# One ring of seven PSUM banks for the attention stages, and their layer norms finished on GpSimd

## The chip, the core and the metric

The kernel runs on one core of one Trainium2 chip. The metric is device time in microseconds (us), the median of several runs. A core has TensorE (PE, the matmuls; its weight loads are shown apart as PEld), VectorE (DVE), ScalarE (ACT), GpSimd (POOL) and SyncE (SP, which here only issues DMAs). The core's PSUM, where matmuls put their results, has eight banks, and a bank holds 128 x 512 float32 numbers, which is one tile of this kernel.

## What is computed

Three transformer layers act on x of shape (4, 512, 288) (batches, tokens, channels), and a rotation stands between the second and the third. Cut to what matters:

```python
h = modulate(layernorm(x), shift, scale)                 # norm 1
q, k, v = split(h @ w_qkv + b_qkv)                       # 16 heads of 18 channels
attn = softmax(einsum('bqhd,bkhd->bhqk', q, k) * 18 ** -0.5)
x = x + gate * (einsum('bhqk,bkhd->bqhd', attn, v).reshape(x.shape) @ w_proj + b_proj)
h = modulate(layernorm(x), shift2, scale2)               # norm 2
x = x + gate2 * mlp(h)       # layer 0: mixture of 4 experts, top 2; layers 1 and 2: one MLP, 288 -> 1152 -> 288
# between layers 1 and 2:
U, _ = qr(P); R = expm(skew(silu(cond) @ W.T + b))
x = x + (x @ U @ R - x @ U) @ U.T
```

The QR factorisation is done by 64 Householder reflections, one after the other.

## The kernel before

**Stages.** Each of the three layers has a start (norm 1, q and k of batch 0, first row maxima), then the attention of four batches, then the MLP of the four batches. Attention and MLP do not overlap except for a few steps at the border.

**A batch of attention.** The 16 heads form four groups of four (g = 0..3), and the 512 keys form four blocks (kt = 0..3), so a batch has 16 steps (g, kt). `walk` sets the order of a step for all engines: two heads' tiles, place A, the other two heads' tiles, place B, the value products, place C. A step has four score tiles (`score_tiles`, L783; ScalarE takes each out with an exp, L1150) and four maximum tiles (`max_tiles`, L770; VectorE reduces each to a row maximum, L1486). The maxima belong to the group after the next (g + 2), so that from g = 2 on they are those of the next batch. The negated maxima are transposed (`turn_maxima`, "R", L697), copied by ScalarE to `nmT`, and written by DMA (L394) as two more rows of `qs`, so that the score matmul itself subtracts the maximum. `value_products` (L794) uses bank 4.

**Other work.** `other_work` lists what stands at the places A, B and C: tiles of q and k of the next batch ("P", five tiles, L683: ScalarE takes the high part out, L1105, VectorE the low part, L1468), v ("V"), transposes of the attention's output ("on", "ot"), the projection ("pj", L734), transposes of normalised tokens ("T1", "T2", L723), the steps of the norms on VectorE ("LN1a" to "LN1h" for the next batch, "LN2a" to "LN2h" for the batch before), and in layer 0 the matrix exponential ("X"), the gate logits, and the reflections ("HH": GpSimd computes, PE sums over partitions, L636, ScalarE copies, L1078, GpSimd goes on, L529 to L540 and L524 to L520). A P tile goes through DRAM: SP stores it (`store_tile`, L369), waits for the store, and loads it in another layout as `qs` and `ks` (`stack`, L386). SP does all of this and the nmT DMAs in one queue, in order.

**Banks.** Scores use banks 2 and 3 in turn, maxima 0, 1 and 5, other work 6 and 7, value products 4. PE waits before a tile until the tile that was last in its bank is read: a score for the exp two scores before, a maximum for the reduction three maxima before, other work for the one two before it. In the MLP banks 0 to 2 and 4 to 7 are used for the hidden and output tiles, and 3 is spare.

**Norms.** A norm on VectorE has 25 instructions: four sums (L1312) and four aggregations (L1315), three to get a first guess of the inverse root, nine Newton steps on 128 x 4 numbers (L1321 to L1323), four normalisations of 128 x 288 (L1330), and a copy of 128 x 384 (L1334), most of them with a wait for the one before.

## Time and profile before

| | us |
|---|---|
| median of 3 runs | 2026.04 (2024.82 to 2034.39) |
| the profiled execution | 2024.0 |
| its span | 2022.2 |
| PE busy | 1818.6 (90%) |
| DVE busy | 1216.9 (60%) |
| ACT busy | 951.0 (47%) |
| POOL busy | 421.2 (21%) |

The span is that of one execution. A busy PE is not PE at its peak: a matmul row also holds the time it spends in the pipeline (0.39 to 0.50 us where the next one starts 0.23 us later), so waits are better read from the distance between the starts of rows than from the busy time. PEclk is the granted clock, 1.00 for 2.4 GHz and 0.50 for 1.2 GHz.

### The profile page before, as it was taken

What the parts mean: (1) busy time and instruction counts of PE and PEld (TensorE: products, weight loads), DVE (VectorE), ACT (ScalarE), POOL (GpSimd) and SP (SyncE); (2) the same over time, 40 slices, a digit from 0 to 9 for tenths busy, and PEclk for the clock granted to TensorE, in tenths of its full rate; (3) what the DMA queues carried; (4) which work ended last, traced back from release to release, by engine and by line L of the source; (5) the groups of instructions that cost most, each with busy time, mean ns of one, the idle gap of its engine ahead of it and who ended that gap; (6) DMA issues with size and microseconds to landing.
All of it is one profiled execution on the core that took longest, in us unless ns stands there. A gap on an engine that the chain in (4) does not pass through costs nothing.

```text
span 2022.2 us, 29597 instructions
## 1 busy us (share of the span) xinstructions
PE 1818.6 (90%) x10184; PEld 1186.3 (59%) x10184; DVE 1216.9 (60%) x2635; ACT 951.0 (47%) x1676; POOL 421.2 (21%) x1066
## 2 busy tenths in 40 slices
PE   5798999998999999999688898989987788888998
PEld 4352445445898998998443444448863344434697
DVE  3654777755455464556576777735546677775544
ACT  2144555555444454444145565564431555556543
POOL 0001444555566663444100000000000000000000
PEclk9678989889999999999688999979996889999899
DMA  6335221203011020100222222111003222221100
GB/s 193 108 86 144 83 61 60 63 22 110 1 31 34 1 65 1 64 1 0 87 66 80 68 70 67 53 62 52 1 1 115 73 64 73 65 80 50 49 13 36
DMA packets 69964, 118.95 MB, mean 59 GB/s; under 512 B 8144, under 2 KB 31451, under 8 KB 69780
## 3 DMA queue, kind: packets, MB, share of 16 engines
q1 hardware_dynamic: 65348, 105.00, 16.5%
q0 software_dynamic: 2064, 8.80, 1.8%
q10 hardware_dynamic: 2416, 3.42, 0.5%
q8 instruction: 74, 1.21, 0.2%
q14 instruction: 62, 0.51, 0.1%
HBM read 85.28 MB, written 31.73 MB: 58 GB/s over the span
## 4 chain that ended last, share of the span: by engine, by line
PE 64%; DVE 12%; DMA 9%; SPq 6%; ACT 4%; issue 4%; POOL 0%; DVEq 0%; ACTq 0%
PE ps L913 17%; PE ps L924 16%; DMA qk_rows<-qk 6%; PE ps L794 6%; PE ps L783 6%; DVE mx L1486 5%; PE ps L683 4%; PE ps L734 3%; SPq L386 3%; ACT pT L1150 2%; PE ps L770 2%; PE ps L723 2%; DMA qs<-nmT 1%; PE ps L690 1%; SPq L394 1%
## 5 line engine op out<-in xcount | busy, mean ns | idle before, releaser
L1486 DVE TENSOR_REDUCE mx<-ps 128x1 f32<-128x512 f32 x768 | 485.5, 682 | 131.0 <-PE ps L770 122.5
L1150 ACT ACTIVATE pT<-ps 128x512 f32<-128x512 f32 x768 | 416.2, 593 | 301.9 <-PE ps L783 295.1
L770 PE MATMUL ps<-ks,qs 54*128 54x512 f32 x768 | 337.7, 523 | 72.9 <-DMA ks<-qk_rows 50.6
L783 PE MATMUL ps<-qs,ks 56*128 56x512 f32 x768 | 319.9, 493 | 62.5 <-ACT pT L1150 35.1
L1432 DVE TENSOR_TENSOR gl<-gf,gh 128x512 fp32r<-128x512 f32 x216 | 149.9, 695 | 272.4 <-ACT gh L1073 269.9
L1072 ACT ACTIVATE gf<-ps,cols 128x512 f32<-128x512 f32 x216 | 148.8, 689 | 339.9 <-PE ps L913 339.5
L783 PEld LDWEIGHTS ps<-qs,ks 56*128 56x128 f32 x768 | 129.1, 197 | 273.4 <-ACT pT L1150 142.2
L924 PE MATMUL ps<-w2h,gh 128*128 128x288 f32 x864 | 255.7, 296 | 1.6 <-DVE tmpx L1519 1.3
L924 PE MATMUL ps<-w2h,gl 128*128 128x288 f32 x864 | 254.7, 295 | 0.0
L924 PE MATMUL ps<-w2l,gh 128*128 128x288 f32 x864 | 254.1, 294 | 0.0
L794 PE MATMUL ps<-pT,vaug 128*32 128x512 f32 x1536 | 228.0, 663 | 0.0
L770 PEld LDWEIGHTS ps<-ks,qs 54*128 54x128 f32 x768 | 136.4, 206 | 121.9 <-DVE mx L1486 64.0
L913 PE MATMUL ps<-hTh,w1h 128*128 128x512 f32 x432 | 177.1, 410 | 1.8 <-DVE w1l L1455 1.7
L913 PE MATMUL ps<-hTl,w1h 128*128 128x512 f32 x432 | 170.9, 396 | 0.0
L913 PE MATMUL ps<-hTh,w1l 128*128 128x512 f32 x432 | 170.8, 395 | 0.0
L924 PEld LDWEIGHTS ps<-w2h,gh 128*128 128x128 f32 x864 | 162.2, 188 | 11.3 <-DVE tmpx L1519 2.2
L924 PEld LDWEIGHTS ps<-w2l,gh 128*128 128x128 f32 x864 | 162.8, 188 | 8.3
L924 PEld LDWEIGHTS ps<-w2h,gl 128*128 128x128 f32 x864 | 162.3, 188 | 0.0
L1073 ACT ACTIVATE gh<-ps,cols 128x512 fp32r<-128x512 f32 x216 | 147.2, 681 | 0.0
L1468 DVE SCALAR_TENSOR_TENSOR qk<-ps,cols,qk 126x512 fp32r<-126x512 f32 (+1 forms) x60 | 44.9, 749 | 87.3 <-ACT qk L1105 86.3
L529 POOL TENSOR_TENSOR hs<-hR,hs 96x1 f32<-96x1 f32 x64 | 39.6, 619 | 275.0 <-ACT hR L1078 275.0
L913 PEld LDWEIGHTS ps<-hTh,w1h 128*128 128x128 f32 x432 | 81.7, 189 | 19.7 <-issue 6.4
(206 smaller groups left out, 2649.0 us busy)
## 6 DMA issues: line engine op xcount, KB each, us to landing
qk_rows<-qk SPq DMA_DIRECT2D x96, 252.0 KB
qs<-qk_rows SPq DMA_DIRECT2D x96, 144.0 KB
ks<-qk_rows SPq DMA_DIRECT2D x96, 144.0 KB
...
```

Of the source, the lines that this page charges most:

```text
L386: sp.dma_start(to[at:at + part.shape[0], i % 2, 2 * g:2 * g + 2, :].bitcast(F32), part).then_inc(S[f"stack_ld{g}"], 16)
L683: ins = mm(ps[0:rows, n, :], w[:, c, o:o + rows], h[:, c, :], start=(c == 0 and k == 0), stop=(c == KC - 1))
L770: ins = mm(bank(MAX_BANKS[v % 3]), qs[at:at + KMAX, buf, h // 2, qt * P:(qt + 1) * P], ks[at:at + KMAX, buf, h // 2, :], start=True, stop= ...
L783: ins = mm(bank(2 + i % 2), ks[at:at + KROW, b % 2, h // 2, kt * P:(kt + 1) * P], qs[at:at + KROW, b % 2, h // 2, :], start=True, stop=Tru ...
L794: ins = mm(ps[32 * i:32 * i + 32, 4, :], vaug[:, kt, g % NG * HG + i, :], pT[:, kt % 2 * HG + i, :], start=(kt == 0), stop=(kt == TT - 1), ...
L913: ins = mm(bank(j % 3), w[:, c, o:o + P], h[:, c, :], start=(c == 0 and n == 0), stop=(c == KC - 1))
L924: ins = mm(ps[:, 4 + t, 0:C], g[:, j % 3, t * P:(t + 1) * P], w[:, j, :], start=(j == 0 and n == 0), stop=(j == NJ - 1 and n == 2))
L1072: A(gf[:, j % 3, :], bank(j % 3), gelu, bias=bias).then_inc(S["gf_done"], 1)
L1073: A(gh[:, j % 3, :], bank(j % 3), gelu, bias=bias).then_inc(S["gh_done"], 1)
L1150: A(pT[:, kt % 2 * HG + i, :], bank(2 + i % 2), ACT.Exp, scale=SCALE).then_inc(S["exp_done"], 1)
L1432: V.tensor_tensor(gl[:, j % 3, :], gf[:, j % 3, :], gh[:, j % 3, :].bitcast(F32), ALU.subtract).then_inc(S["gl_done"], 1)
L1486: V.tensor_reduce(mx[:, g % NG, qt, column(i):column(i) + 1], bank(MAX_BANKS[(NU * g + qt * HG + i - first) % 3]), AX.X, ALU.max).then_inc ...
```

## The change

- **Banks.** `banks()` hands out the seven banks 6, 7, 0, 1, 5, 2, 3 in one ring to scores, maxima and other work, in the order in which PE issues them. A tile waits for the reader of the tile seven takes before, whatever it was. The end of a layer's attention uses 5, 6, 7.
- **Norms.** Within attention VectorE keeps `bn_stats` and `bn_aggr` (`statistics`). GpSimd does the rest (`normalise`): add epsilon, power -0.5, two products on 128 x 4, four 128 x 288 `tensor_scalar`, the copy of 128 x 384. These are 18 norms: norm 1 of batches 1 to 3 and norm 2 of batches 0 to 2, in each layer. Norm 1 of batch 0 and norm 2 of batch 3 stay on VectorE.
- **GpSimd's order.** In layer 0 it now walks through the same places as the others, so reflections, norms and the issue of three weight loads stand in that order. Reflections in attention are at steps 0, 2, 5, 7, 10, 12 and 14 of batches 1 and 2 and at the first six of these in batch 3 (20 in all; before at every even step, 24), and the third expert gets three a batch where it had two.
- **Tiles of q and k.** P2 stays at step 8 (g = 2, kt = 0), P3 moves from step 12 to 11, P4 from step 0 of the next batch to step 15; for batch 0 P4 is computed in the start, among the maxima.
- **Negated maxima.** They are laid out so that two DMAs of two rows each replace four of one row.
- The wait for all readers (`all_read`) at the end of a start is gone.

```diff
-FWD_KT = (0, 2)
-FWD_J = ((1, 4, 7), (1, 4, 7), (2, 6), (2, 6))
-FWD_AT = (B - 1) * NG * len(FWD_KT)
+FWD_STEP = ((), (0, 2, 5, 7, 10, 12, 14), (0, 2, 5, 7, 10, 12, 14), (0, 2, 5, 7, 10, 12))
+FWD_J = ((1, 4, 7), (1, 4, 7), (1, 4, 7), (2, 6))
+FWD_AT = sum(len(s) for s in FWD_STEP)
...
+def banks():
+    table, ring, n = {}, [0], [AROUND]
+    def take(phase, kind, key):
+        table[phase, kind, key] = n[0][ring[0] % len(n[0])]
+        ring[0] += 1
...
+            def tile(g, kt, which):
+                for i in which:
+                    take(phase, "score", (g, kt, i))
+                    if g + 2 < NG or b + 1 < B:
+                        take(phase, "max", (g + 2, kt, i))
...
-MAX_BANKS = (0, 1, 5)
+AROUND = (6, 7, 0, 1, 5, 2, 3)
+BANK = banks()
...
-                    for row in range(2):
-                        for e in range(2):
-                            at = HALF * e + KMAX + row
-                            sp.dma_start(qs[at:at + 1, G // NG % 2, 2 * g:2 * g + 2, :].bitcast(F32),
-                                         nmT[HG * row + 2 * e:HG * row + 2 * e + 2, :].bitcast(F32)).then_inc(S[f"nm_ld{g % 2}"], 16)
+                    for e in range(2):
+                        at = HALF * e + KMAX
+                        sp.dma_start(qs[at:at + 2, G // NG % 2, 2 * g:2 * g + 2, :].bitcast(F32), nmT[HG * e:HG * e + HG, :].bitcast(F32)).then_inc(S[f"nm_ld{g % 2}"], 16)
...
+            def normalise(which, i, b, eps, xn_free):
...
+                pool.wait_ge(S[f"mv{which}_ready"], TT * done)
+                ordered(g.tensor_scalar(var, mvp[:, which - 1, :, 1], eps, 1.0, ALU.add, ALU.mult))
+                ordered(g.tensor_tensor(y, var, power[:, :].to_broadcast([P, TT]), ALU.pow))
+                ordered(g.tensor_tensor(w, mean, y, ALU.mult))
+                ordered(g.tensor_scalar(w, w, -1.0, 1.0, ALU.mult, ALU.mult))
...
+                for t in range(TT):
+                    g.tensor_scalar(xn[:, t, 0:C], xres[:, b * TT + t, :], y[:, t:t + 1], w[:, t:t + 1],
+                                    ALU.mult, ALU.add).then_inc(S[f"xn{which}_ready"], 1)
...
-                        pe.wait_ge(S["exp_done"], G * NU + (NU * g + kt * HG + i + 1))
+                        n = bank_free("score", (g, kt, i), "exp_done", G * NU + (NU * g + kt * HG + i + 3))
...
-                            layernorm(1, it + 1, b + 1, EPS[l], kind[3], (S["tr2_done"], it * KC + KC))
+                            statistics(1, it + 1, b + 1, kind[3])
```

On PE, in a step without other work (layer 1, batch 1, g = 3, kt = 2), where L783 is a score, L770 a maximum and L794 the value products; before:

```order
L783 MATMUL ps<-qs,ks 128x512 [waits exp_done]
L770 MATMUL ps<-ks,qs 128x512 [waits mx_done]
L783 MATMUL ps<-qs,ks 128x512 [waits exp_done]
L770 MATMUL ps<-ks,qs 128x512 [waits mx_done]
L783 MATMUL ps<-qs,ks 128x512 [waits exp_done]
L770 MATMUL ps<-ks,qs 128x512 [waits mx_done]
L783 MATMUL ps<-qs,ks 128x512 [waits exp_done]
L770 MATMUL ps<-ks,qs 128x512 [waits mx_done]
L794 MATMUL ps<-pT,vaug 32x512 [waits exp_done]
```

and the same step after, where L880, L867 and L891 are the same three (on_ready is VectorE's division of the attention's output, nmT_ready ScalarE's copy of the maxima):

```order
L880 MATMUL ps<-qs,ks 128x512 [waits mx_done]
L867 MATMUL ps<-ks,qs 128x512 [waits nmT_ready]
L880 MATMUL ps<-qs,ks 128x512 [waits exp_done]
L867 MATMUL ps<-ks,qs 128x512 [waits mx_done]
L880 MATMUL ps<-qs,ks 128x512 [waits exp_done]
L867 MATMUL ps<-ks,qs 128x512 [waits mx_done]
L880 MATMUL ps<-qs,ks 128x512 [waits on_ready]
L867 MATMUL ps<-ks,qs 128x512 [waits exp_done]
L891 MATMUL ps<-pT,vaug 32x512 [waits exp_done]
```

The matmuls and their order are the same; what each waits for is now the tile seven takes back, of either kind or of other work.

On VectorE, in steps 1 and 2 of the same batch (L1486 is a maximum, L1498 a tile of v, L1315 and the rest the norm); before:

```order
L1498 TENSOR_TENSOR vaug<-ps,vbias 128x16x18 [waits pv_done,v_mm]
L1315 BN_AGGR mv<-stats 128x2 x4
L1316 TENSOR_SCALAR nwt<-mv 128x4 [waits ln1_step]
L1318 TENSOR_SCALAR nwt<-nwt 128x4 [waits ln1_step]
L1319 TENSOR_SCALAR nwt<-nwt 128x4 [waits ln1_step]
L1486 TENSOR_REDUCE mx<-ps 128x1 [waits ln1_step,max_mm]
L1486 TENSOR_REDUCE mx<-ps 128x1 [waits max_mm]
L1498 TENSOR_TENSOR vaug<-ps,vbias 128x16x18 [waits pv_done,v_mm]
L1321 TENSOR_TENSOR nwt<-nwt 128x4
L1322 SCALAR_TENSOR_TENSOR nwt<-nwt 128x4 [waits ln1_step]
L1323 SCALAR_TENSOR_TENSOR nwt<-nwt 128x4 [waits ln1_step]
L1486 TENSOR_REDUCE mx<-ps 128x1 [waits ln1_step,max_mm]
```

and after, where L1614 is the tile of v, L1450 the aggregation and L1601 the maximum:

```order
L1614 TENSOR_TENSOR vaug<-ps,vbias 128x16x18 [waits pv_done,v_mm]
L1450 BN_AGGR mvp<-stats 128x2 [waits ln1_step,xc1_ready]
L1450 BN_AGGR mvp<-stats 128x2 x3
L1601 TENSOR_REDUCE mx<-ps 128x1 [waits max_mm] x2
L1614 TENSOR_TENSOR vaug<-ps,vbias 128x16x18 [waits pv_done,v_mm]
L1601 TENSOR_REDUCE mx<-ps 128x1 [waits max_mm] x2
```

The small steps between the maxima are gone from VectorE's queue.

On GpSimd, in batch 1 of layer 0, after the change (L594 to L604 are the norm, L567 and L568 begin the next reflection, whose end is not shown):

```order
L594 TENSOR_SCALAR nwp<-mvp 128x4 [waits mv2_ready]
L595 TENSOR_TENSOR nwp<-nwp,power 128x4 [waits lnp_step]
L596 TENSOR_TENSOR nwp<-mvp,nwp 128x4 [waits lnp_step]
L597 TENSOR_SCALAR nwp<-nwp 128x4 [waits lnp_step]
L601 TENSOR_SCALAR xn<-xres,nwp 128x288 [waits tr1_done,tr2_done,lnp_step]
L601 TENSOR_SCALAR xn<-xres,nwp 128x288 x3
L604 COPY xn<-xn 128x4x96 [waits xn2_ready]
L567 TENSOR_TENSOR hs<-hR,hs 96x1 [waits hh_cp]
L568 TENSOR_SCALAR hs<-hR 96x1 [waits hh_step]
```

Before, the reflections followed each other there with nothing between them.

## Rows read from the trace of the kernel before

**Rows 1.** Windows: layer 0 batch 1, its MLPs; layer 1 start and four batches.
```profile
core 0: us, PE busy (x) PEld busy (x) DVE busy (x) ACT busy (x) POOL busy (x), PEclk, DMA share, GB/s
...
196.70:295.80 99.10, 93.49 (x569) 47.33 (x565) 74.07 (x174) 52.47 (x101) 46.07 (x124) 0.93 0.29 84
...
520.00:960.00 440.00, 437.00 (x2590) 391.81 (x2589) 237.87 (x458) 200.50 (x335) 239.15 (x580) 1.00 0.07 23
966.60:1016.80 50.20, 30.23 (x79) 16.60 (x78) 30.64 (x56) 8.63 (x12) 0.22 (x2) 0.62 0.30 96
1016.80:1103.60 86.80, 73.98 (x404) 34.94 (x404) 58.40 (x131) 45.77 (x83) 0.00 (x0) 0.86 0.25 77
1103.60:1186.60 83.00, 72.91 (x411) 34.98 (x411) 65.09 (x150) 48.59 (x89) 0.00 (x0) 1.00 0.24 73
1186.60:1274.90 88.30, 78.63 (x411) 37.12 (x411) 65.37 (x150) 48.60 (x89) 0.00 (x0) 0.92 0.21 68
1274.90:1345.00 70.10, 63.65 (x326) 27.55 (x326) 37.05 (x85) 42.56 (x79) 0.00 (x0) 0.87 0.19 63
```

**Rows 2.** Timeline of PE, end of layer 1 batch 1: start us, us, engine line.
```profile
1178.64 0.50 PE L783 MATMUL ps<-qs,ks 56*128 56x512 f32 x1
...
1178.99 0.39 PE L783 MATMUL ps<-qs,ks 56*128 56x512 f32 x1
1179.83 0.50 PE L783 MATMUL ps<-qs,ks 56*128 56x512 f32 x1 [0.45 <-ACT pT L1150]
...
1180.75 1.07 PE L794 MATMUL ps<-pT,vaug 128*32 128x512 f32 x8
1181.75 0.49 PE L783 MATMUL ps<-qs,ks 56*128 56x512 f32 x1
...
1186.62 0.50 PE L783 MATMUL ps<-qs,ks 56*128 56x512 f32 x1 [1.71 <-DMA qs<-nmT]
```

**Rows 3.** Waits over the whole span: us in total, times, longest us.
```profile
PE ps L770 <- DMA ks<-qk_rows: 50.6, 12, 10.9
...
PE ps L783 <- ACT pT L1150: 35.1, 66, 1.4
...
PE ps L770 <- DVE mx L1486: 22.0, 33, 1.3
```

**Rows 4.** VectorE's groups in layer 1 batch 1: busy us, mean ns, idle before.
```profile
L1486 DVE TENSOR_REDUCE mx<-ps 128x1 f32<-128x512 f32 x64 | 40.7, 683 | 4.7 <-PE ps L770 3.4
...
L1330 DVE TENSOR_SCALAR xn<-xres,mv,nwt 128x288 f32<-128x288 f32 x8 | 3.0, 423 | 0.2 <-DVE nwt L1323 0.2
...
L1322 DVE SCALAR_TENSOR_TENSOR nwt<-nwt 128x4 f32<-128x4 f32 x6 | 1.0, 163 | 0.9 <-DVE nwt L1321 0.3
...
L1334 DVE COPY xn<-xn 128x384 f32<-128x384 f32 x2 | 0.7, 360 | 0.1
```

**Rows 5.** Chain that ended last, end of layer 1 batch 1: start us, us, what.
```profile
1171.43 1.85 PE ps L683 x7
...
1174.90 4.82 DMA qk_rows<-qk
...
1182.79 0.64 SPq L394
...
1184.71 1.87 DMA qs<-nmT
```

**Rows 6.** Timeline of GpSimd, one reflection in layer 0 batch 2.
```profile
301.66 0.55 POOL L529 TENSOR_TENSOR hs<-hR,hs 96x1 f32<-96x1 f32 x1 [3.64 <-ACT hR L1078]
...
305.66 0.46 POOL L510 TENSOR_TENSOR hp<-hr,hvc 96x165 f32<-96x165 f32 x1
...
308.42 0.30 POOL L520 TENSOR_TENSOR hr<-hp 96x55 f32<-96x55 f32 x1
```

**Rows 7.** VectorE's groups: MLP of layer 0 (GpSimd busy), then layer 1 (idle).
```profile
L1432 DVE TENSOR_TENSOR gl<-gf,gh 128x512 fp32r<-128x512 f32 x125 | 86.6, 694 | 155.6 <-ACT gh L1073 155.2 <-DVE stats L1312 0.2
...
L1432 DVE TENSOR_TENSOR gl<-gf,gh 128x512 fp32r<-128x512 f32 x30 | 20.7, 691 | 47.1 <-ACT gh L1073 47.1
```

236 lines of the change are left out of this document (156 added, 80 removed), and 9 rows, old and new, of the table own.

## The prediction

> **What bounds the kernel now.** First the windows by stage [rows 1]. In the MLPs of layer 0 TensorE is busy 437 of 440 us at the full clock, with a quarter of VectorE's time to spare: nothing there can be gained by this change, and the MLPs of the other layers look the same. In attention the row of layer 1, batch 1 is the one to read, because its clock is 1.00 throughout: 83.0 us, TensorE busy 72.9, VectorE 65.1, ScalarE 48.6. No engine is full, and 72.9 is an upper figure, since a matmul's row holds pipeline time. Batch 2 does the same work in 88.3 us at a clock of 0.92; batch 3, which prepares no next batch, takes 70.1.
>
> Why no engine is full is seen in a step that has nothing but tiles and value products [rows 2]. Two scores, with a maximum beside each, start at 1178.64 and 1178.99, so a pair costs TensorE 0.35 us. The third score starts at 1179.83, not at 1179.34: it waited for the exp that reads its bank. The next step starts at 1181.75, so the step took 3.11 us. TensorE's own part is 4 x 0.35 + 1.00 (value products, 1180.75 to 1181.75) = 2.40 us. VectorE's part is four reductions of 40.7 / 64 = 0.64 us [rows 4], 2.54 us. So the step costs 0.57 us more than its busiest engine needs. The two banks of the scores are what couples them. In the list of waits the same shows as 35.1 us behind exps and 22.0 us behind reductions [rows 3]; both understate it, since the row of the matmul before covers part of each wait.
>
> The third kind of wait is for DMA: 50.6 us for ks, 12 times, up to 10.9 us [rows 3], and 1.71 us at the border of batches 1 and 2, for the negated maxima [rows 2]. Its chain [rows 5]: P3 starts at 1171.43, its store is on its way from 1174.90 for 4.82 us, then come the loads, and at 1182.79 the first of four nmT DMAs, each 0.6 us of SP; the last lands at 1186.58. From P3 to the score are 15.2 us.
>
> **Part 1, the ring of banks.** Nothing is added: the matmuls and their order stay. In a bare step a score may now run 3.5 pairs ahead of the exps instead of 2, and a maximum about as far as before. Both ends: all of the 0.57 us in each of 16 steps, 9.1 us a batch; or nothing in the steps with other work, where ScalarE and VectorE catch up meanwhile, which leaves about 5 bare or nearly bare steps, 2.9 us. Steps with other work also stall today, so I take a value above the middle of 2.9 and 9.1: 6.1 less 0.6 for steps that VectorE or ScalarE fill by themselves (T1, the residuals), 5.5 us. Nine batches (0 to 2 of each layer): 49.5 us. Batch 3 has half its maxima and waits mostly for exps: 5 us each, 15 us. Sum 64.5, between 26 + 6 and 82 + 27.
>
> The coupling is new in one respect: a score may wait for a reduction, and a maximum for an exp. VectorE's queue is the longer one, 65.1 us a batch against 48.6 [rows 1], so scores could be held by it. This is where part 2 helps.
>
> **Part 2, the norms.** VectorE loses per batch eight normalisations (3.0 us), two copies (0.7), eighteen Newton steps (18 x 0.16 = 2.9) and six other small ones of about the same length (1.0) [rows 4]: 7.6 us, which leaves 57.5. It also loses the waits between them (0.9 us before L1322). On the path this is worth little beyond part 1, which already lets the waits for reductions go. Between 0 and 2.4 us a batch (22.0 us of waits over nine batches), I take 0.5: 4.5 us.
>
> GpSimd's price has no row of its own. A tensor_tensor of 96 x 165 takes 0.46 us and one of 96 x 55 0.30 us [rows 6], so 1.45 ns for an element more and 0.64 us for 288; for the copy of 384, 0.78 us. The power takes about the 0.55 us of L529, which is one; the three other small steps at most as much. A norm is then 4 x 0.64 + 0.78 + 4 x 0.55 + 0.4 for waits = 5.9 us. It starts at place C of step 1 and is needed by T1 at step 4, two steps later, 2 x 83.0 / 16 = 10.4 us now and 9.4 if the batch shrinks to 75; norm 2 has from step 7, place B, to step 9, place C. In layer 0 a reflection stands ahead of it in GpSimd's queue: 301.66 to 308.72, 7.1 us [rows 6]. With the 1 us until ScalarE's copy that is 7.1 + 1 + 5.9 = 14.0 us from place B of step 0, against 3.5 steps of 99.1 / 16 = 6.2 us, 21.7 us. So the norm costs nothing on the path. If the cover were gone each microsecond over it would cost 9 us a norm kind.
>
> Do the two engines hinder each other? VectorE's L1432 reads two SBUF tensors and takes 694 ns where GpSimd works beside it and 691 ns where it is idle [rows 7]. That is no hindrance. The Trainium skill (SBUF — State Buffer, "Who interferes with whom") says that a VectorE instruction with two SBUF inputs and a GpSimd instruction that reads SBUF lock each other out for a whole instruction. The row does not bear it out for GpSimd's short steps; by the rule some eleven such VectorE instructions a batch would each lose at most one 0.64 us GpSimd instruction, 7 us, and part 2 would give VectorE nothing. The skill also calls GpSimd the wrong place for elementwise work, about twice as slow for two inputs (GPSIMD Engine Reference, "4.1 Engine selection"); from VectorE's 0.42 us [rows 4] that is 0.85 us an instruction and 6.9 us a norm, which the cover still holds.
>
> **Part 3, P3, P4 and two DMAs for four.** P3 starts a step earlier (3.1 us) and SP issues two nmT DMAs fewer (2 x 0.6 = 1.2 us). Together they exceed the 1.71 us of the border's wait [rows 2]; what is late next is VectorE. Nine borders, 1.3 us each (the others wait less or more): 12 us, between 0 and 15. A P tile costs TensorE 1.85 us [rows 5] wherever it stands; only in a start does moving it pay. There the clock is 0.62 [rows 1], so P4 costs 3 us or more, and it now lies among maxima, where VectorE is the slow one. With the 1.2 us of DMA issues: 4 us, three starts, 12 us (3 to 15).
>
> **Part 4, what comes back.** The chain from P1 to the maxima of the next batch is of the same kind as that from P3, 15 us, and nothing shortens it. P1 is in step 5 and its load is needed in step 8. As steps 5 to 7 get shorter TensorE arrives sooner and waits longer for ks; in batch 0 all that these steps gain is lost. I put 2 us on each of nine batches, with the slower clock after such a wait: -18 us (0 to -40).
>
> **Reflections.** The attention has 20 for 24 and a spacing of 2 or 3 steps for 2; the third expert has a reflection each 10 us, as the first two have today in the 437 of 440 us [rows 1]. No cost.
>
> **Sum.** 64.5 + 4.5 + 12 + 12 - 18 = 75 us. The profiled execution took 2024.0 us (span 2022.2); 1949 us. The median of three is 2 us above that execution: 1951 us.
>
> **Rivals.**
> *More comes back through the clock.* The same work cost 5.3 us more at 0.92 than at 1.00 [rows 1]. If fewer waits keep the clock up, about 4 us more in ten batches, and part 1 at its upper end: 1951 - 45 = 1906 and below.
> *DMA takes over.* Steps 8 to 11 and 11 to 15 shrink too, and the chains of P2 and P3 (15 us each) become the pace: four steps at 3.8 us are 15.2 us. Then two more places in each of nine batches wait for 2 us: 1951 + 36 = 1987. For it: 50.6 us are waited for ks already. Against: only batch 0 waits long.
> *It doesn't do what it says.* The chain is PE, exp, value products, and the ring only moves the wait to the exps that the value products need: then only part 3 is left, 2 to 10 us, about 2018.
> *Slower: the clock falls.* The wait before a maximum is spread today; if it gathers at the DMA waits, the 1.2 GHz stretch that follows each of them in the starts (clock 0.62) comes in every batch. At 5.3 us for 0.08 of clock, ten batches at 0.78 in place of 0.92 cost 93 us, against the 75 gained: about 2044. It decides from a mean clock in attention below about 0.81.
>
> **How the numbers follow.** Forecast (1915 to 1975) 0.61; more through the clock (1880 to 1915) 0.10; DMA takes over (1975 to 2012) 0.16; no effect 0.06; slower 0.07. The range 1903 to 1993 leaves out most of the first rival's far half, the far half of the second, and the last two. A measurement can tell about 0.5%, 10 us, from no change. Faster by more: 0.61 + 0.10 + 0.16 = 0.87; within: 0.06; slower: 0.07.
>
> **What would show it.** A batch at full clock of 74 to 77 us for 83.0. A bare step of 2.6 to 2.8 us for 3.11, bound by reductions that follow each other without a gap. VectorE's busy time in such a batch near 57.5 us, and GpSimd with two norms of about 6 us. The border's wait gone. The wait for ks larger than 50.6 us. MLPs unchanged. The prediction is wrong if PE waits for xn at T1, if VectorE's reductions get longer than 0.68 us beside GpSimd, or if the clock in attention is lower than now.

## The result, and the profile after

The changed kernel takes 1898.45 us (median of 4 runs, 1893.26 to 1903.29) where the kernel before took 2025.43 us beside it (2018.41 to 2034.39): a ratio of 0.937, 95% interval 0.9326 to 0.9415. It is 127 us faster, where 75 were forecast; the direction was right, and the time lies 4.5 us below the low end of the range, 1903. The profiled execution has a span of 1896.5 us and a mean granted clock of 0.942, where the kernel before had 2022.2 us and 0.923.

First the page of the changed kernel: busy time and share of each engine, with the number of instructions. GpSimd has 81 us more than before, VectorE 68 us less, TensorE 95 us less, though its matmuls in attention are the same; the granted clock is higher, and how much of the 95 us is clock and how much is waiting inside its rows was not separated.

```profile
PE 1723.5 (91%) x10184; PEld 1165.3 (61%) x10184; DVE 1148.8 (61%) x2329; ACT 940.4 (50%) x1676; POOL 502.0 (26%) x1229
```

Windows of the changed kernel, the same stretches as in [rows 1]: the MLPs of layer 0, then layer 1: the start and its four batches. Columns: busy us (and instructions) of PE, PEld, DVE, ACT, POOL, then the granted clock.

```profile
510.00:945.00 435.00, 430.55 (x2570) 388.19 (x2568) 234.82 (x452) 197.80 (x331) 262.85 (x642) 1.00 0.07 23
945.00:993.80 48.80, 26.50 (x84) 15.96 (x84) 30.09 (x54) 9.30 (x13) 0.00 (x0) 0.66 0.30 99
993.80:1069.10 75.30, 68.93 (x406) 35.42 (x406) 54.31 (x114) 44.16 (x83) 4.41 (x9) 0.88 0.29 89
1069.10:1140.90 71.80, 69.31 (x417) 34.31 (x413) 57.66 (x117) 47.86 (x90) 8.78 (x18) 1.00 0.26 84
1140.90:1212.80 71.90, 69.18 (x415) 34.22 (x411) 57.54 (x117) 47.74 (x90) 8.78 (x18) 1.00 0.26 84
1212.80:1269.20 56.40, 52.68 (x322) 24.60 (x320) 31.81 (x68) 37.30 (x73) 4.39 (x9) 0.94 0.20 66
```

The row to compare is again batch 1 of layer 1, with a clock of 1.00 on both sides: 83.0 us have become 71.8. That is 11.2 us at the same clock, where the terms of the sum came to 5.3 (5.5 + 0.5 + 1.3 - 2). Batch 2 fell further, 88.3 to 71.9, since its clock also went from 0.92 to 1.00.

A bare step of that batch, PE and then VectorE (start us, us, engine, line; L880 is a score, L867 a maximum, L891 the value products, L1601 a reduction):

```profile
1134.11 0.50 PE L880 MATMUL ps<-qs,ks 56*128 56x512 f32 x1
1134.11 0.73 PE L867 MATMUL ps<-ks,qs 54*128 54x512 f32 x2
...
1135.73 1.06 PE L891 MATMUL ps<-pT,vaug 128*32 128x512 f32 x8
1136.72 0.50 PE L880 MATMUL ps<-qs,ks 56*128 56x512 f32 x1
...
1134.68 3.30 DVE L1601 TENSOR_REDUCE mx<-ps 128x1 f32<-128x512 f32 x5 [0.19 <-PE ps L867]
```

From 1134.11 to 1136.72 are 2.61 us, for 3.11 in [rows 2], and the five reductions follow each other without a gap. No wait for an exp is left in the step.

GpSimd's norm 1 in the same kernel, and then what TensorE waited for over the whole span (us in total, times, longest), PE's rows first and then three of the weight loads (L880 is a score, L867 a maximum):

```profile
1078.68 0.19 POOL L594 TENSOR_SCALAR nwp<-mvp 128x4 f32<-128x4 f32 x1 [69.77 <-DVE mvp L1450]
1078.95 1.02 POOL L595 TENSOR_TENSOR nwp<-nwp,power 128x4 f32<-128x4 f32 x1
...
1080.65 2.27 POOL L601 TENSOR_SCALAR xn<-xres,nwp 128x288 f32<-128x288 f32 x4
1082.99 0.50 POOL L604 COPY xn<-xn 128x384 f32<-128x384 f32 x1
```

```profile
PE ps L867 <- DMA ks<-qk_rows: 59.8, 13, 10.9
PE ps L880 <- DMA qs<-nmT: 19.1, 5, 7.1
PE ps L824 <- POOL xn L601: 5.4, 3, 2.0
PEld ps L880 <- DVE mx L1601: 34.3, 66, 0.8
PEld ps L880 <- ACT pT L1251: 19.7, 29, 1.1
PEld ps L867 <- DVE mx L1601: 15.3, 48, 0.7
```

The norm takes 4.8 us from 1078.68 to 1083.49 (5.9 forecast). The wait for ks has grown from 50.6 us [rows 3], and TensorE waits three times for GpSimd's xn, once in batch 3 of each layer. Now that all share a ring, the weight loads of scores wait for reductions too (34.3 us), which none did before; this is the new coupling that the prediction named.

### The profile page after: what moved, and what is told of

Its sections match the earlier page's. It is cut to its first block, busy times and chain, and to the rows that moved or that the text cites. A ratio compares the mean times of both kernels' runs of the same rounds, so it can differ in the third digit from the quotient of the medians.

```text
span 1896.5 us, 29159 instructions
## 1 busy us (share of the span) xinstructions
PE 1723.5 (91%) x10184; PEld 1165.3 (61%) x10184; DVE 1148.8 (61%) x2329; ACT 940.4 (50%) x1676; POOL 502.0 (26%) x1229
## 4 chain that ended last, share of the span: by engine, by line
PE 71%; DMA 9%; DVE 6%; ACT 5%; SPq 4%; issue 3%; POOL 2%; ACTq 0%; DVEq 0%; POOLq 0%
PE ps L1014 18%; PE ps L1025 17%; PE ps L891 6%; PE ps L880 6%; DMA qk_rows<-qk 6%; PE ps L784 4%; PE ps L867 3%; PE ps L791 3%; SPq L426 2%; PE ps L835 2%; DVE mx L1601 2%; ACT pT L1251 1%; PE ps L805 1%; DMA ks<-qk_rows 1%; PE ps L824 1%
## 5 line engine op out<-in xcount | busy, mean ns | idle before, releaser
L1601 DVE TENSOR_REDUCE mx<-ps 128x1 f32<-128x512 f32 x768 | 482.4, 681 | 96.6 <-PE ps L867 94.5
L1251 ACT ACTIVATE pT<-ps 128x512 f32<-128x512 f32 x768 | 409.4, 598 | 242.7 <-PE ps L880 241.8
L867 PE MATMUL ps<-ks,qs 54*128 54x512 f32 x768 | 292.0, 491 | 62.8 <-DMA ks<-qk_rows 59.8
L880 PE MATMUL ps<-qs,ks 56*128 56x512 f32 x768 | 272.7, 462 | 21.8 <-DMA qs<-nmT 19.1
L880 PEld LDWEIGHTS ps<-qs,ks 56*128 56x128 f32 x768 | 119.4, 194 | 182.0 <-issue 107.2
L891 PE MATMUL ps<-pT,vaug 128*32 128x512 f32 x1536 | 214.2, 624 | 10.0 <-ACT pT L1251 10.0
L594 POOL TENSOR_SCALAR nwp<-mvp 128x4 f32<-128x4 f32 x18 | 3.5, 195 | 824.9 <-DVE mvp L1450 824.8
L867 PEld LDWEIGHTS ps<-ks,qs 54*128 54x128 f32 x768 | 124.4, 202 | 97.8 <-DMA ks<-qk_rows 64.8
L567 POOL TENSOR_TENSOR hs<-hR,hs 96x1 f32<-96x1 f32 x64 | 39.2, 612 | 208.5 <-ACT hR L1179 208.5
L1014 PEld LDWEIGHTS ps<-hTh,w1l 128*128 128x128 f32 x432 | 81.9, 190 | 19.8
```

The costliest lines, as they stand in the source:

```text
L867: ins = mm(bank(n), qs[at:at + KMAX, buf, h // 2, qt * P:(qt + 1) * P], ks[at:at + KMAX, buf, h // 2, :], start=True, stop=True, tile_posi ...
L880: ins = mm(bank(n), ks[at:at + KROW, b % 2, h // 2, kt * P:(kt + 1) * P], qs[at:at + KROW, b % 2, h // 2, :], start=True, stop=True, tile_ ...
L891: ins = mm(ps[32 * i:32 * i + 32, 4, :], vaug[:, kt, g % NG * HG + i, :], pT[:, kt % 2 * HG + i, :], start=(kt == 0), stop=(kt == TT - 1), ...
L1014: ins = mm(bank(j % 3), w[:, c, o:o + P], h[:, c, :], start=(c == 0 and n == 0), stop=(c == KC - 1))
L1251: A(pT[:, kt % 2 * HG + i, :], bank(BANK[when[0], "score", (g, kt, i)]), ACT.Exp, scale=SCALE).then_inc(S["exp_done"], 1)
L1601: V.tensor_reduce(mx[:, g % NG, qt, column(i):column(i) + 1], bank(BANK[when[0], "max", (g, qt, i)]), AX.X, ALU.max).then_inc(S["mx_done"], 1)
```

## Where the time went, by batches

From the trace of each kernel the first score of every batch was taken, and for the end of batch 3 the first matmul of the MLP; the sums of the three layers are below, in us. The kernels between are experiments, told of below; from row to row one part is added (with the norms also the new places of the reflections and the start without `all_read`, which no run takes apart). It is one execution of each kernel; the ratios, given with the experiments, differ from this by up to some 9 us in a step.

| | batch 0 (3) | batches 1, 2 (6) | batch 3 (3) | all |
|---|---|---|---|---|
| before | 282.4 | 543.0 | 225.9 | 1051.3 |
| + norms on GpSimd (e4) | 279.9 | 499.2 | 228.3 | 1007.4 |
| + places of P, two DMAs (e1) | 269.6 | 484.9 | 219.2 | 973.7 |
| + scores and maxima share five banks (e15) | 266.0 | 486.2 | 199.1 | 951.3 |
| + all seven in one ring (changed kernel) | 259.8 | 467.5 | 195.0 | 922.3 |

The norms give 44 us, the places and DMAs 34, the sharing of five banks 22, the ring of seven 29: 129 us together. About 2.4 us of it are given back in the third expert of layer 0, which has a reflection more in each batch (eight matmuls in all). Its windows, before and then after, have their PE columns beside a clock of 1.00:

```profile
728.90:846.60 117.70, 117.70 (x702) 106.25 (x701) 64.03 (x119) 53.36 (x89) 54.05 (x130) 1.00 0.09 28
...
704.10:824.20 120.10, 118.76 (x710) 107.13 (x709) 63.87 (x118) 54.75 (x93) 77.57 (x193) 1.00 0.09 28
```

## Experiments: the parts alone and taken away

All ratios are to the kernel before on the same chip; 0.01 is 20 us. The changed kernel has 0.937. Theory A said that the ring carries the gain, theory B that ring and relieved VectorE need each other.

**Old banks.** In `banks()`, each kind has its own banks again:

```diff
-        table[phase, kind, key] = n[0][ring[0] % len(n[0])]
+        own = {"score": (2, 3), "max": (0, 1, 5)}.get(kind, (6, 7))
+        table[phase, kind, key] = own[used[own] % len(own)]
```

> The changed kernel with the banks dealt out as before: scores on 2 and 3, maxima on 0, 1 and 5, other work on 6 and 7; norms on GpSimd and all else as changed. Theory A (the ring carries the gain, the rest is small): 2000 us or more, that is over 100 us slower than the changed kernel, and a full-clock batch of 81 to 83 us for 71.8. Theory B (ring and relieved VectorE need each other; each alone gives a part): 1960 to 1990 us, batch at 76 to 80. By the prediction's own terms (64.5 us for the ring) 1963 us. A bare step of about 3.1 us again by all of them.

Measured: 1954.37 us, ratio 0.9621 (0.9597 to 0.9645). The whole ring is worth 51 us as the last part to be added (0.9621 - 0.937 = 0.0251). That is the prediction's term less a fifth, and half of what theory A wanted; what the ring loses again by later waits for ks (part 4 of the prediction) is inside the 51. The batch 1 of layer 1 takes 74.8 us, not 81.

**Norms on VectorE.** `on_gpsimd` gives False, `layernorm` with its parts a to h stands at its old places, `normalise` is not called.

> The changed kernel with the 18 norms of attention wholly on VectorE, in the places that they had before; the ring and all else as changed. Theory A: 1903 to 1915 us, since the norms were priced at 0.5 us a batch. Theory B: VectorE's 7.6 us a batch come back nearly whole, as its reductions are what the steps wait for once the ring is there: 9 x 5 to 7.6 us, plus clock, 1945 to 1975 us, with waits for mx and a batch of 77 to 79 us.

Measured: 1962.57 us, ratio 0.9642 (0.9616 to 0.9668). The norms are worth 55 us as the last part, where 4.5 were forecast. Theory A falls here. In its trace TensorE also waits for VectorE's xn, 16.1 us in 8 places (7.9 us in 9 places in the kernel before, none in that of the norms alone, below).

**The ring alone, and the norms alone.** The first has the edit of e2, the old places of P3 and P4 and four DMAs; the second the old banks, places and DMAs.

> The ring of seven banks alone: norms on VectorE, P3 at step 12, P4 at step 0 of the batch itself, four one-row DMAs for the negated maxima, all as before; only the reflections stand at their new steps. Theory A: 1925 us or less (over 100 of the 127 us gained). Theory B: 1955 to 1985 us. By the prediction's terms 2024 - 64.5 = 1960 us.

> The norms on GpSimd alone: banks, places of P3 and P4 and the four DMAs as before. Theory A: 2015 to 2025 us. Theory B: 1995 to 2012 us, since the waits for reductions (22 us) and the serial steps of the norm go. By the prediction's terms 2020 us.

Measured: the ring alone 2003.13 us, ratio 0.9868 (0.984 to 0.9896), 27 us; the norms alone 1980.56 us, ratio 0.9742 (0.9724 to 0.976), 52 us. Both theories thought too well of the ring, and both too little of the norms alone. Of the ring alone, batch 3, which has no norm 1 and few maxima, has 23.6 us (225.9 to 202.3); the six batches in the middle have 8 (543.0 to 534.9). Theory B is right in that much of the ring's gain there needs the norms gone, and wrong in that the norms need no ring: they give 52 us by themselves.

**P3 and P4 at their old places, four DMAs for two.** The first puts P3 back to step 12 and P4 to step 0, with SyncE's order that belongs to them (its edit is not shown); the second is:

```diff
-                        at = HALF * e + KMAX
-                        sp.dma_start(qs[at:at + 2, ...], nmT[HG * e:HG * e + HG, :])
+                        for r in range(2):
+                            at = HALF * e + KMAX + r
+                            sp.dma_start(qs[at:at + 1, ...], nmT[HG * e + 2 * r:HG * e + 2 * r + 2, :])
```

> The changed kernel with P3 at step 12 and P4 at step 0 of the batch itself again (and SyncE's order that belongs to them); ring, norms on GpSimd and two DMAs as changed. Theory C (the places are worth what they showed beside the old banks, where norms alone gave 1981 us and norms with new places 1954 us): 1925 to 1935 us, steps 0, 12 and 15 of a batch longer by about 4 us together. Theory D (by the prediction's term, 1.3 us a border and 3 of the 4 us of a start): 1898 + 12 + 9 = 1919 us or less.

> The changed kernel with four one-row DMAs for the negated maxima instead of two of two rows. Theory C: 1904 to 1912 us, 1.2 us more at a border where the maxima are late and in a start, hidden elsewhere. Theory D: 1898 to 1903 us.

Measured: old places 1939.23 us, ratio 0.9562 (0.9513 to 0.9611), 39 us; four DMAs 1911.17 us, ratio 0.9412 (0.9366 to 0.9459), 9 us, which is not clear of noise, since this interval overlaps with that of the changed kernel. Beside the ring the places are worth more than both theories gave them: in the trace of e5 TensorE waits 45.3 us in 16 places for qs<-nmT, and 19.1 in 5 places in the changed kernel. Beside the old banks, from e4 to e1, places and DMAs together are worth 0.0121, 25 us, by the ratios the forecast of 24 (34 us by the single traces above).

## Experiments: why the norms were worth so much

The prediction held 22.0 us of waits behind reductions [rows 3] for an upper bound. The wait list has PE's rows and PEld's rows, and only the first were read. The weight load of the same maximum stands in the page of the kernel before with three times as much (idle time and what ended most of it, at the end of the line), and so does that of a score:

```profile
L770 PEld LDWEIGHTS ps<-ks,qs 54*128 54x128 f32 x768 | 136.4, 206 | 121.9 <-DVE mx L1486 64.0
L783 PEld LDWEIGHTS ps<-qs,ks 56*128 56x128 f32 x768 | 129.1, 197 | 273.4 <-ACT pT L1150 142.2
```

Neither number is a price. The 22.0 us count too little, since the matmul before covers part of a wait; the weight loads' rows count too much: scores wait 142.2 us for exps there, and the ring alone (e3), which leaves 21.5 us of it, gave 27 us. The price has to be read in the steps.

Step 9 of layer 1, batch 1, before, shows what happens: two weight loads of maxima on PEld, and VectorE in the same stretch.

```profile
1158.02 0.18 PEld L770 LDWEIGHTS ps<-ks,qs 54*128 54x128 f32 x1 [1.05 <-DVE mx L1486]
...
1160.82 0.18 PEld L770 LDWEIGHTS ps<-ks,qs 54*128 54x128 f32 x1 [1.55 <-DVE mx L1486]
```

```profile
1157.27 1.29 DVE L1486 TENSOR_REDUCE mx<-ps 128x1 f32<-128x512 f32 x2
1158.48 0.15 DVE L1321 TENSOR_TENSOR nwt<-nwt 128x4 f32<-128x4 f32 x1
1158.78 0.16 DVE L1322 SCALAR_TENSOR_TENSOR nwt<-nwt 128x4 f32<-128x4 f32 x1
1159.09 0.17 DVE L1323 SCALAR_TENSOR_TENSOR nwt<-nwt 128x4 f32<-128x4 f32 x1
1159.40 0.77 DVE L1330 TENSOR_SCALAR xn<-xres,mv,nwt 128x288 f32<-128x288 f32 x2 [0.15 <-DVE nwt L1323]
1160.09 1.28 DVE L1486 TENSOR_REDUCE mx<-ps 128x1 f32<-128x512 f32 x2
```

VectorE is never idle for long in this step (at most 0.15 us at a time), while both maxima wait for its reductions: it sets the step's length, though over the batch it is busy for 65 of 83 us. And a Newton step costs 0.31 us from start to start (1158.48, 1158.78, 1159.09, 1159.40), not the 0.16 us of its row; the rest is spent with the wait for its own end. Three experiments take the pieces apart, as far as they go. Theory E counts VectorE's work in the steps with a norm, theory F the small steps that wait; theory G says that the time from start to start is what is paid, theory H that the norm's result came too late.

**Only the small steps moved.** GpSimd computes the root and the two factors; VectorE keeps the four normalisations and the copy of each norm.

```diff
+                    if part == "g":
+                        dve.wait_ge(S[f"nw{which}_ready"], sum(on_gpsimd(which, k) for k in range(i + 1)))
+                        dve.wait_ge(*xn_free)
+                    if part in "gh":
+                        for t in (0, 1) if part == "g" else (2, 3):
+                            V.tensor_scalar(xn[:, t, 0:C], xrow(b, t), nwp[:, which - 1, 1, t:t + 1], nwp[:, which - 1, 2, t:t + 1],
+                                            ALU.mult, ALU.add).then_inc(S[f"xn{which}_ready"], 1)
...
```

> The changed kernel with only the steps on 128 x 4 numbers of each norm on GpSimd; the four normalisations of 128 x 288 and the copy of 128 x 384 (3.7 us a batch for both norms) stay on VectorE in their old places. With all of the norm on VectorE it was 1963 us, with none 1898. Theory E (what counts is VectorE's work in the steps where the norm stands, 2 to 4 and 8 to 9): about half of the 64 us come back, 1920 to 1935 us. Theory F (what counts are the Newton steps, each waiting for the one before, that hold the reductions behind them): 1898 to 1910 us.

Measured: 1903.87 us, ratio 0.937 (0.932 to 0.9419), the same as the changed kernel. By the time theory F holds: moving the 3.7 us a batch of large instructions gave nothing that can be told from no change. But the trace shows that two things cancel. The six middle batches take 477.5 us (467.5 in the changed kernel), and TensorE waits 10.2 us in 11 places for VectorE's xn; batch 3 takes 187.2 us (195.0), about as in e16 below (185.2), where GpSimd starts norm 2 earlier. So the large instructions need not be free.

**Small steps added to VectorE, with and without waits.** In both kernels `statistics` got, at the places of the old guess and Newton steps:

```diff
+                    if part in "cdef":
+                        for n in range(3):
+                            at = 3 * "cdef".index(part) + n
+                            V.tensor_tensor(tiny[:, which - 1, at, :], nwt[:, 0, :], nwt[:, 0, :], ALU.mult).then_inc(ln, 1)
+                            wait_alone(dve, ln, steps_before(which, i) + TT + at + 1, S["dve_passed"])
```

The last line is left out in the second.

> The changed kernel plus 12 multiplications of 128 x 4 per norm on VectorE, each with a wait for its own end, at the places where the changed-over norm had its start guess and Newton steps; results unused, output the same. Theory G (the time is VectorE's, and it counts from start to start, 0.31 us an instruction with the wait, in steps where VectorE is the slowest engine): 24 x 0.31 = 7.4 us a batch, nine batches, 50 to 65 us more than the changed kernel, 1950 to 1962 us. Theory H (the cost of the norm on VectorE came from its result being late, not from the time it takes): below 1915 us.

> The same 24 small multiplications a batch without any wait between them. If only their own work counts (0.06 to 0.16 us each) 1.4 to 3.8 us a batch, 1911 to 1932 us; if the wait between dependent instructions is what costs, it is at the lower end of this or below; if the wait costs nothing, the same as with waits.

Measured: with waits 1944.76 us, ratio 0.9556 (0.9509 to 0.9603), 38 us more than the changed kernel; without waits 1904.81 us, ratio 0.936 (0.9314 to 0.9406), no difference that can be told. VectorE's rows, three small instructions in one, first without and then with waits; the last row is what follows behind the waits, started by the end of the last small one:

```profile
1081.91 0.29 DVE L1456 TENSOR_TENSOR tiny<-nwt 128x4 f32<-128x4 f32 x3
```

```profile
1097.70 0.77 DVE L1456 TENSOR_TENSOR tiny<-nwt 128x4 f32<-128x4 f32 x3
1098.69 0.46 DVE L1621 TENSOR_TENSOR vaug<-ps,vbias 128x288 f32<-128x288 f32 x1 [0.22 <-DVE tiny L1456]
```

Three with waits hold VectorE for 0.99 us (1097.70 to 1098.69), three without for 0.29. This is theory G's direction with three quarters of its lowest price: 38 us of the 55 that the norms are worth, by work whose result nobody needs. So theory H cannot be the whole: 38 us come without any late result. It has a part, though, since with the norms on VectorE beside the ring (e2) TensorE waits 16.1 us for xn, and e9 has no more than the changed kernel there (5.5 us for GpSimd's). That is near the other 17 us, but no run takes it apart from the large instructions, which also come back in e2.

Theory G, that VectorE's time from start to start is all that is paid, isn't shown either: a part of the 38 us goes through TensorE's clock. In layer 1, batch 1, TensorE waits twice for work of VectorE (0.29 and 0.79 us at 1099.2 and 1100.7), and what follows runs at a granted clock of 0.50, 1.2 GHz. Windows of e9, whose profiled run is the longest of its four (1952.6 us): up to this point, the slow stretch, and the rest of the batch:

```profile
1083.10:1101.40 18.30, 17.07 (x104) 9.26 (x100) 16.36 (x45) 10.72 (x21) 4.39 (x9) 0.97 0.22 65
1101.40:1110.60 9.20, 9.20 (x38) 3.48 (x37) 4.78 (x10) 5.36 (x9) 0.00 (x0) 0.50 0.01 3
1110.60:1164.80 54.20, 51.39 (x281) 25.00 (x277) 40.71 (x88) 32.48 (x60) 4.40 (x9) 0.94 0.30 89
```

9.2 us of uninterrupted matmuls at 0.50 are 4.6 us more than at 1.00 (an estimate), of the 9.9 us by which this batch is longer than in the changed kernel (81.7 for 71.8); its mean clock is 0.90 for 1.00. What VectorE costs without the clock is cleaner from the kernel before to e4, both at 1.00 in this batch: 83.0 to 76.4 us.

The Trainium skill (VectorE: DVE Perf Modes, "The DRAIN you can't avoid") reports that a semaphore after each of eight copies costs nothing over one after the last. The rows here do not agree for instructions on 128 x 4: 0.33 us each with a wait, 0.10 without.

## Experiments: how long a norm may take on GpSimd

**The norm made longer.** The four normalisations are written five times:

```diff
+                for again in range(4):
+                    for t in range(TT):
+                        ordered(g.tensor_scalar(xn[:, t, 0:C], xres[:, b * TT + t, :], y[:, t:t + 1], w[:, t:t + 1], ALU.mult, ALU.add))
```

> The changed kernel with the four normalisations on GpSimd written five times instead of once (16 more of 0.58 us and their waits, about 10 to 11 us; the norm goes from 4.4 to about 15 us); output the same. The cover was worked out as 9.4 to 10.4 us outside layer 0. If that is right TensorE waits 4 to 6 us at T1 and at T2 of each batch, 1960 to 2010 us in all. If the cover is much longer than worked out (GpSimd may run far ahead) it stays below 1920 us. If GpSimd's work hinders VectorE through the shared memory, VectorE's reductions get longer than the 680 ns of now.

Measured: 2068.47 us, ratio 1.0188 (1.0138 to 1.0238): slower than the kernel before, and worse than the upper end of what was expected. GpSimd and TensorE in layer 1, batch 1:

```profile
1139.30 0.20 POOL L594 TENSOR_SCALAR nwp<-mvp 128x4 f32<-128x4 f32 x1 [66.67 <-DVE mvp L1453]
...
1152.23 2.27 POOL L604 TENSOR_SCALAR xn<-xres,nwp 128x288 f32<-128x288 f32 x4
...
1154.65 1.08 PE L827 MATMUL ps<-ident,xn 128*128 128x128 f32 x4 [7.16 <-POOL xn L604]
```

The window of this batch, as in [rows 1]:

```profile
1129.90:1221.60 91.70, 77.14 (x413) 37.86 (x415) 57.97 (x117) 48.50 (x89) 27.49 (x50) 0.85 0.21 66
```

TensorE stood ready at 1154.65 - 7.16 = 1147.5, which is 8.2 us after the norm had begun. The cover was worked out as 9.4 us for a batch of 75 us, and the batch is shorter, 71.8 us, which makes it 9.0. In the whole run TensorE waits 122.4 us for xn, and the clock of the batch is 0.85. VectorE's busy time in the batch stays at 57.97 us beside 27.5 us of GpSimd (57.66 beside 8.78). That is not to say that the two engines never hold each other up; the rows for this are in the part on why the prediction was wrong.

## Experiments: what of the ring gives the gain

The ring gave 17 us in the six middle batches and 24 in batch 3 (e1 to the changed kernel), where 5.5 and 5 us each, so 33 and 15, were forecast. Theory J says that scores lacked room, theory K that sharing is what gives.

> The changed kernel with fixed banks again, but dealt otherwise: scores on 2, 3 and 5, maxima on 0 and 1, other work on 6 and 7. With scores on two and maxima on three it was 1954 us. Theory J (what the ring gave is room for scores: three banks instead of two): 1905 to 1925 us, batch 3 at 57 to 60 us. Theory K (sharing gives it, since maxima lose what scores win): batches 0 to 2 as long as with the old banks or longer, 1930 us or more, batch 3 alone shorter.

> The changed kernel with a ring of the five banks 6, 7, 0, 1, 2 (5 and 3 unused in attention). Theory J: five shared banks are a lead of 2.5 pairs, more than the two of the old score banks: 1905 to 1930 us. Theory K': other work in the ring eats the lead in the steps that have it, so that five banks are no better than seven in three fixed parts: 1945 us or more.

> The changed kernel with scores and maxima sharing 0, 1, 5, 2 and 3 in one ring, other work on 6 and 7 as before. If the sharing of other work matters little: within 8 us of the changed kernel, 1898 to 1906 us. If other work was held by its two banks (P, T1 and the projection stand close together in steps 4 and 5): 1910 us or more, with longer steps 4 and 5.

Measured: three score banks and two for maxima 1997.96 us, ratio 0.9839 (0.9787 to 0.9891); a ring of five for everything 1968.86 us, 0.9694 (0.9644 to 0.9744); scores and maxima sharing five, other work with its two 1928.97 us, 0.9495 (0.9446 to 0.9543). The old banks had 0.9621. Theory J is wrong: a third bank for scores at the cost of a maximum's makes the kernel slower by 0.0218, 44 us. The lengths of steps 0 to 15 in layer 1, batch 1, from the starts of the scores, with a clock of 1.00 in the first, second, third, fourth and last:

```
before           5.3 4.7 5.8 5.1 5.2 11.8 5.4 3.6 6.2 6.8 3.9 3.3 4.2 3.8 3.1 4.9
norms alone, e4  5.3 4.7 5.0 3.7 4.3 11.9 5.4 3.6 5.0 4.4 3.9 3.4 4.2 3.8 3.1 4.8
old banks, e1    4.7 4.6 5.0 3.7 4.3 11.8 5.5 3.6 4.6 4.4 3.9 4.2 3.6 3.8 3.1 4.1
five shared, e15 4.7 4.6 5.0 3.7 4.3 11.9 5.5 3.6 4.6 4.4 3.9 4.2 3.6 3.8 3.1 4.1
ring of five,e14 4.7 4.9 4.9 3.9 4.6 14.0 5.5 3.6 4.6 5.0 3.9 4.5 3.6 3.9 3.1 4.2
changed          3.7 4.9 4.9 3.5 4.1 11.4 5.4 2.6 5.8 4.4 3.5 4.2 2.6 4.0 2.6 4.1
```

Three readings. From the first line to the second, steps 2, 3, 4, 8 and 9 shrink by 0.8, 1.4, 0.9, 1.2 and 2.4 us, 6.7 in all, and no other by more than 0.1: these are the steps in which the norm stood, or the one right behind it. From the third to the fourth nothing changes: five banks in one ring are no better than two and three, as long as scores and maxima come in pairs. When other work is in the ring of five too (e14), step 5, where P0, P1 and a projection stand, takes 2.2 us more; the clock of that step is 0.88, so most of it may be clock, and the 40 us between e14 and e15 are not read from it. Only seven banks in the ring shorten the bare steps, 3.1 to 2.6, and step 0, 4.7 to 3.7. Theory K is right only about batch 3. There the kernel has no maxima from step 8 on, so fixed banks leave three of seven idle. Windows of batch 3 of layer 1, in e1 and then in e15, where the clock rises too, from 0.89 to 0.97 (at most 0.11 x 68.1 - 0.03 x 57.3 = 5.8 of the 10.8 us, an estimate):

```profile
1239.50:1307.60 68.10, 62.10 (x324) 26.90 (x320) 34.03 (x71) 42.10 (x79) 4.39 (x9) 0.89 0.20 64
```

```profile
1227.80:1285.10 57.30, 53.94 (x323) 25.09 (x319) 32.13 (x69) 37.75 (x74) 4.40 (x9) 0.97 0.20 64
```

## A version that is faster than both

In the changed kernel the longest waits are those of batch 0 at step 8. Its chain of waits there in layer 1 (start us, us, what):

```profile
1021.78 1.64 PE ps L784 x7
...
1025.01 5.42 DMA qk_rows<-qk
...
1030.49 0.30 SPq L426
...
1033.15 3.60 DMA ks<-qk_rows
```

P1 starts at 1021.78, its rows are in DRAM at 1030.43, eight loads are issued and the last lands at 1036.75: 15.0 us, the same as the 15.2 of [rows 5]. Two edits of `other_work`:

```diff
-            (2, "A", [("V", 2)]), (2, "C", [("V", 3)])],
+            (2, "A", [("V", 2)]), (2, "C", [("V", 3)]), (3, "B", [("T1", 0)]), (3, "C", [("T1", 1)])],
-        1: [(0, "A", [("T1", 0)]), (0, "B", [("T1", 1)]), (0, "C", [("T1", 2)]), (1, "A", [("P", 0)]), (1, "B", [("P", 1), ("pj", 0)]),
+        1: [(0, "A", [("T1", 2)]), (0, "B", [("P", 0)]), (0, "C", [("P", 1)]), (1, "B", [("pj", 0)]),
...
-            (1, "C", [("pj", 1)]), (2, "A", [("pj", 2), ("pj", 3)]), (2, "C", [("LN2a", 0)]), (3, "A", [("LN2b", 0)]), (3, "B", [("LN2c", 0)])],
+            (1, "C", [("pj", 1)]), (2, "A", [("pj", 2), ("LN2a", 0), ("pj", 3)]), (2, "C", [("LN2b", 0)]), (3, "A", [("LN2c", 0)])],
```

The first (with SyncE's stack of group 0 ahead of its maxima) is e11, the second e16, both are e12.

> The changed kernel with the transposes of norm 1 at places B and C of step 3 and A of step 4 (before: A, B, C of step 4), P0 and P1 at B and C of step 4 (before: A and B of step 5), and in SyncE's queue the stack of group 0 ahead of the negated maxima of group 2. If the chain from P1 to ks is what step 8 waits for (5.8 to 7.5 us in batches 1 and 2, 13.2 to 14.6 us in batch 0, where 3.9 are its work), step 8 falls to 4 us in batches 1 and 2 and by 6 us or more in batch 0: 1850 to 1875 us. Theory D' (the negated maxima, now behind eight loads, are late instead): 1890 us or more, with waits for nmT at step 8.

> As the kernel before this one, and the sums of norm 2 one place earlier each (at A and C of step 6 and A of step 7), so that GpSimd starts it one place earlier. In batch 3 TensorE waited 5.4 us in all for GpSimd's xn at step 9: 3 to 10 us less than the kernel before this one. If the residuals hold VectorE there, no difference.

> The changed kernel with only the sums of norm 2 one place earlier each. With the earlier T1, P0 and P1 besides it was 1888 us, with these alone 1897. If the gain is norm 2's alone: 1886 to 1892 us, batch 3 shorter by about 3 us in each layer, the others unchanged.

Measured: e11 1896.73 us, ratio 0.9329 (0.9282 to 0.9375); e16 1893.46 us, 0.931 (0.9257 to 0.9363); e12 1887.99 us, 0.9279 (0.9233 to 0.9325). The last is faster than the changed kernel by about 0.9 points; the upper end of its interval, 0.9325, lies just below the lower end of the changed kernel's, 0.9326. e16 and e11 by themselves overlap with it. The earlier norm 2 does what was expected of it: from its start to its last score batch 3 falls from 56.4 us in the changed kernel to 51.7 in e16 in layer 1 and from 55.0 to 51.7 in layer 2. The earlier P tiles were a miss. The wait for ks falls as thought, here in e12:

```profile
PE ps L869 <- DMA ks<-qk_rows: 37.8, 5, 11.2
PE ps L882 <- DMA qs<-nmT: 22.6, 8, 7.8
```

But the 22 us less of it gave 6 to 8 us (0.931 to 0.9279, and 0.937 to 0.9329). In batch 0 of layer 1 step 8 fell from 13.2 to 6.1 us and step 7 grew from 2.9 to 5.4; in batches 1 and 2 of that layer steps 3 to 5 grew by about 1 us. Step 8 takes 4.6 to 4.7 us in the four middle batches of layers 1 and 2 of e12, for 5.8, 6.1, 7.5 and 5.3 in the changed kernel and 7.5, 9.2, 5.5 and 8.0 in e16. So 1.5 us of it on average were waiting in one trace and 2.9 in the other; the prediction's 2 us for each batch lies between.

## Why the prediction was wrong

**What bounds the kernel.** The bare step was read rightly, and it came out at the low end of what was forecast, 2.61 us for 2.6 to 2.8. What was not read is that the steps with a norm have another bound, VectorE, though [rows 1] show it with time to spare over the batch. A mean of 65 in 83 us hides five steps in which it sets the pace.

**Part 2 is the step that failed.** It was worth 0.5 us a batch, 4.5 in all, "little beyond part 1, which already lets the waits for reductions go". The runs say 52 us alone and 55 as the last part beside the ring. Two readings failed. The bound of 2.4 us a batch came from 22.0 us of PE's waits for reductions, which is not a bound: 64.0 us stood in the weight loads, and in the steps with a norm the reductions behind it set the pace (6.6 us of the 83.0 in layer 1, batch 1, at a clock of 1.00). And the Newton steps were costed at 0.16 us, while they hold VectorE for 0.31; the prediction names the 0.9 us of idle time before L1322 [rows 4] and puts no price on it. What this price is made of is shown in part: 38 us by small steps that wait (e9), some of it through the clock; the rest, by waits for a late xn or by the large instructions, stays open. What was said of GpSimd held: 4.8 us a norm for 5.9 (0.58 us for 128 x 288 where 0.64 was estimated, 0.50 for the copy where 0.78 was), no wait at T1. The power was the exception, 1.02 us for 0.55. The cover ran out in one place that had not been worked out, norm 2 of batch 3, where the steps are shorter: 5.4 us in all.

**Parts 1 and 4** have to be taken together, since each measured value of the ring holds its later waits for ks: 64.5 - 18 = 46.5 us, beside 51 measured (e1). By batch the forecast is then 5.5 - 2 = 3.5 us for batches 0 to 2, beside 2.9 in the middle (17.4 / 6) and 3.3 in batch 0, and 5 us for batch 3 beside 8. In layer 1, batch 1, the steps other than 8 shrink by 4.2 us from e1 to the changed kernel, where 5.5 were forecast, and step 8 grows by 1.2. So part 1 was somewhat too high for the full batches and too low for batch 3: the row said that half the maxima are missing there, and the prediction didn't ask what the banks of the missing ones would do. That the sum came out near is luck in this respect. The wait for ks rose by 9.2 us (50.6 to 59.8); in the traces of e10 and e16 it is 63.3 and 64.6.

**Part 3** was 24 us: 25 beside the old banks, 39 and 9 as the last parts beside the ring. The shorter the steps, the more the border's wait for qs<-nmT is worth.

**Reflections** were costed at nothing and took 2.4 us in the third expert (1.1 us of TensorE busy, 1.3 us idle, from the two windows above): TensorE was full there, so that each matmul added lengthens the stage. The same paragraph of the prediction gives VectorE a quarter of its time to spare in that stage; 237.87 of 440 us leave nearly half. Nothing hangs on it.

**The rivals.** The time lies inside the first rival's, 1906 and below, but its mechanism is the smaller part. (Its own terms, 10 x 4 for the clock and 44.5 for part 1 at its upper end, are 85 us and not 45.) At an unchanged clock of 1.00 the batch is 11.2 us shorter. The four middle batches of layers 1 and 2 lost 57.1 us, where 4 x 11.2 are 44.8: some 12 us there (an estimate, with the 11.2 us of one batch for all four) go with the clock that was at 0.92 or so before and is near 1.00 now. DMA did not take over: in layer 1, batch 1, steps 12 and 0, where P2's and P3's loads are needed, take 2.6 and 3.7 us; the ring is not without effect; the clock did not fall. e8 shows how that last rival would have come about, by the norm and not by DMA: with 7 us of waits at T1 the clock of the batch goes to 0.85 and the kernel is slower than before.

**Do the two engines hinder each other?** The prediction said no, from 694 beside 691 ns [rows 7], and this reading was wrong: the 694 are a mean over 125 instructions. In the trace the 51 of them that meet no GpSimd instruction take 694 ns at most; of the 74 that meet one, eight take more than 700, up to 809, and the rest are as short as the others. In the whole trace of the kernel before the longest takes 877. A pair of normalisations that takes 0.77 us at 1159.40, where GpSimd is idle, takes 1.32 us beside reflections in layer 0; VectorE, then GpSimd:

```profile
218.84 1.32 DVE L1330 TENSOR_SCALAR xn<-xres,mv,nwt 128x288 f32<-128x288 f32 x2
...
218.91 0.49 POOL L510 TENSOR_TENSOR hp<-hr,hvc 96x186 f32<-96x186 f32 x1
219.48 0.51 POOL L540 TENSOR_TENSOR hA<-hA,hp 96x186 f32<-96x186 f32 x1
```

In the changed kernel a small step (L1608) from 218.94 takes 0.45 us where it otherwise takes 0.18, and ends at 219.39, when GpSimd's instruction of 218.85 has ended at 219.36:

```profile
218.94 0.45 DVE L1608 SCALAR_TENSOR_TENSOR nm<-mx,nm 128x16 fp32r<-128x16 f32 x1
...
218.85 0.51 POOL L578 TENSOR_TENSOR hA<-hA,hp 96x186 f32<-96x186 f32 x1
```

The reductions, which read PSUM, are untouched: 680 ns in the batch (683 in [rows 4]) and 682 ns in e8, with three times GpSimd's work. The Trainium skill (SBUF — State Buffer, "Who interferes with whom") says the same of both: a lock between VectorE and GpSimd for a whole instruction, and none for VectorE's reductions on this chip. So the reductions, which the prediction took as its sign, could not have shown the lock. What was wrong in the prediction is the price by the rule, 7 us a batch: beside GpSimd's 72 normalisations in the changed kernel the trace has three VectorE instructions that read nothing but SBUF, all in layer 0 and none of the eleven that the prediction counted, and VectorE's busy time came out at 57.66 us where 57.5 were forecast.

The Trainium skill (GPSIMD Engine Reference, "4.1 Engine selection") has twice VectorE's time for instructions with two inputs, and about the same time for one input. The normalisation has one tensor as input and takes 0.58 us on GpSimd and 0.42 on VectorE, 1.4 times: between the two. The prediction's 6.9 us for a norm (6.8 by its own terms) used the rule for the other kind, and 4.8 were measured.
